# Second-layer keys made in the second attention from turned contexts kept in memory

## What is computed

```
x = x + tanh(g_xattn[0]) * attention0(layernorm(x), ctx)    # keys and values: context and own rows, masked
x = x + tanh(g_ffn[0])   * block0(layernorm(x))             # 8-bit rounding of rows and weights
x = x + tanh(g_xattn[1]) * attention1(layernorm(x), ctx)    # keys and values: context only
x = x + tanh(g_ffn[1])   * experts(layernorm(x))            # 2 of 8 experts a token, 256 -> 1024 -> 256
```

## Time and profile before

| | |
|---|---|
| median of 3 runs | 618.8 us (612.36 to 625.53) |
| profiled execution | 618.93 us |
| its span, first to last instruction | 617.2 us |
| busy: PE, DVE, ACT, POOL | 493.9, 424.3, 302.2, 162.2 us |
| first attention, steps of rounds 0 to 7 | 54.8 to 239 us |
| second attention, steps of rounds 0 to 7 | 328 to 438.8 us |
| bytes read and written in memory | 48.59 and 15.92 MB |

### The profile page before, as it was taken

How to read it: one execution, slowest core, us unless ns; L and a number is a source line. 1 busy time by engine, 2 the same in 40 slices (tenths; PEclk the granted TensorE clock), 3 DMA queues, 4 the chain that set the end, 5 groups by cost and what they waited for, 6 DMA issues and landing times. The chain is left out here.

```text
span 617.2 us, 15503 instructions
## 1 busy us (share of the span) xinstructions
PE 493.9 (80%) x5419; PEld 348.6 (56%) x5419; DVE 424.3 (69%) x920; ACT 302.2 (49%) x499; POOL 162.2 (26%) x191
## 2 busy tenths in 40 slices
PE   3987888898898877665478989999663299999993
PEld 2565566666565565333234656666443287887882
DVE  8767867777677754777528768877469776566651
ACT  5557565556555374143344757776542133333331
POOL 4600211221222111120245111101231425545432
PEclk9997999999999779786586989999775599999998
DMA  9577654454376000000467999994383012222210
GB/s 256 132 140 144 183 127 107 117 141 94 85 171 181 5 27 1 1 1 0 115 118 193 169 164 180 173 159 154 106 308 123 25 36 36 41 47 40 46 21 0
DMA packets 73247, 64.31 MB, mean 104 GB/s; under 512 B 33326, under 2 KB 65750, under 8 KB 73190
## 3 DMA queue, kind: packets, MB, share of 16 engines
q1 hardware_dynamic: 62904, 41.68, 31.3%
q0 software_dynamic: 8224, 21.06, 13.7%
q10 hardware_dynamic: 2064, 0.81, 0.5%
HBM read 48.59 MB, written 15.92 MB: 105 GB/s over the span
## 5 line engine op out<-in xcount | busy, mean ns | idle before, releaser
L518 PEld LDWEIGHTS PS<-QS,KS 112*120 112x120 f16 (+2 forms) x896 | 81.0, 140 | 28.8 <-issue 10.7
L518 PE MATMUL PS<-QS,KS 112*120 112x100 f16 (+2 forms) x896 | 89.2, 224 | 7.5 <-ACT QS L590 5.5
L629 DVE CUSTOM_DVE_ANT_0 PS<-PS,maskv 100x461 f32<-100x461 f32 x118 | 74.3, 647 | 14.7 <-PE PS L480 14.3
L632 DVE TENSOR_REDUCE mx<-PS 100x1 f32<-100x361 f32 x128 | 63.8, 529 | 30.0 <-PE PS L483 28.4
L581 ACT ACTIVATE PT<-PS 120x400 f32<-120x400 f32 (+1 forms) x128 | 63.3, 502 | 42.6 <-PE PS L518 41.5
L581 ACT ACTIVATE PT<-PS,ctxb 120x400 f32<-120x400 f32 (+1 forms) x96 | 56.9, 594 | 32.1 <-PE PS L518 30.9
L861 POOL TENSOR_SCALAR_AFFINE_SELECT PT<-PT 100x400 f32<-100x400 f32 x32 | 17.3, 541 | 159.9 <-ACT PT L581 159.9
L2173 PE MATMUL PS<-aT,WE 128*128 128x128 f16 x960 | 59.1, 223 | 0.0
L2173 PEld LDWEIGHTS PS<-aT,WE 128*128 x960 | 56.7, 100 | 0.1
L480 PE MATMUL PS<-KS,QS 65*100 65x461 f16 x118 | 44.9, 381 | 12.9 <-DVE mx L629 12.6
L2186 PE MATMUL PS<-WE,hidden_high 128*128 x160 | 53.0, 379 | 0.0
(11 more groups left out here) (322 smaller groups left out, 1050.2 us busy)
## 6 DMA issues: line engine op xcount, KB each, us to landing
share<-in_L_ffn_w_dram POOLq DMA_DIRECT2D x13, 1024.0 KB, 9.1
k_scratch<-share SPq DMA_DIRECT2D x32, 180.5 KB, 2.7
KS<-k_scratch SPq DMA_DIRECT2D x32, 180.5 KB, 3.9
KS<-k_scratch SPq DMA_DIRECT2D x64, 90.2 KB, 8.0
QS<-q_scratch SPq DMA_DIRECT2D x64, 50.0 KB, 2.8
v_scratch<-xn SPq DMA_DIRECT2D x8, 385.7 KB
values_staged<-v_scratch SPq DMA_DIRECT2D x8, 385.7 KB
WE<-in_L_ffn_w_dram POOLq DMA_DIRECT2D x2, 1024.0 KB, 8.7
```

What stands on the lines that cost most here:

```text
L518: last = nc.tensor.matmul(bank[0:kn, i * T:(i + 1) * T], KS[p][:, h, k0:k0 + kn], QS[p][:, h, :], start=True, stop=True)
L629: nc.vector.tensor_tensor_reduce(rows, rows, maskv[:, :], 1.0, -BIG, ALU.add, ALU.max, mx[p][:, h:h + 1]).then_inc(s_smf, 1)
L632: nc.vector.tensor_reduce(mx[p][:, h:h + 1], sm_bank[h % 2][0:T, 0:TC], X, ALU.max).then_inc(s_smf, 1)
```

## The change

The turned contexts (both halves, 361 KB a batch) are written to memory in the first attention, where the second layer's keys were written. In the first attention K2 and K3 are gone from set-up and rounds 0 to 5. For batches 0 and 1, whose second-layer keys must be there before the second attention, the turned context is read back into `cT[0]`, and the keys are made in round 6 (t=4, 5) and round 7 (t=1, 2). For batches 2 to 7 they are made in rounds 0 to 5 of the second attention, at t=0 and t=4, with ACT's half behind t=2 and t=5 and DVE's half behind the fifth and the eleventh maximum, from one buffer `cK`. SP writes them, waits until they have landed, and loads them back into the stack. Unread products are issued in these rounds only from t=8 on. Several tiles have new places. The loops over rounds are shorter by one turn in the second attention, with that turn's two rounds written out.

```diff
-        NV0, NK0, NW0 = 4, (2, 3, 6, 7), 8
-        TVK = {1: "T0", 2: "T1", 4: "K0", 5: "K1", 8: "V0", 9: "V1", 11: "K2", 12: "K3"}
+        NV0, NK0, NW0 = 4, (2, 3), 6
+        TVK = {1: "T0", 2: "T1", 4: "K0", 5: "K1", 8: "V0", 9: "V1"}
...
+        K17 = (1, 2)
...
+        def pe_K1b(pe, b, mb, n):
+
+            if mb == 0:
+                pe.wait_ge(s_c1, 16 * (b + 1))
+            pe.wait_ge(s_mf, n - 1)
+            pe_second_keys(pe, misc[KB[mb]][:, 0:TC], cT[0], mb).then_inc(s_md, 1)
...
         def act_hi_T(act, j, o, kc, n):
+            if o >= 2 and kc == 0:
+                act.wait_ge(s_cw[o % 2], 16 * (j + o // 2))
...
+        def sp_turned_out(sp, j, o):
+
+            sp.dma_start(c_dram[bass.ds(2 * j + o, 1)].rearrange("b p n -> (b p) n"),
+                         cT[o % 2][:, :, :, :].rearrange("p r k t -> p (r k t)")).then_inc(s_cw[o % 2], 16)
...
                     if keys:
+                        sp_turned_out(sp, j, u + 2)
...
-                        sp.wait_ge(s_mf, n0 + NK0[3] + 1)
-                        sp_keys_out(sp, j, u + 2, 1)
...
-                for p in range(2):
-                    sp.wait_ge(s_kw[1][p], KW * B // 2)
-                sp.dma_start(rd_[:, :, 0:NI], w_down.rearrange("(k p) n -> p k n", p=P)).then_inc(s_fw, 16)
-                round0(B // 2 - 1, 0, False, False, True)
+                sp.wait_ge(s_mf, N6)
+                sp.wait_ge(s_cw[0], 16 * B // 2)
+                sp_turned_in(sp, slice(0, 1), cT[0], s_c1)
+                sp.dma_start(rd_[:, :, 0:NI], w_down.rearrange("(k p) n -> p k n", p=P)).then_inc(s_fw, 16)
+                sp.wait_ge(s_mf, N6 + 2)
+                sp.wait_ge(s_cw[1], 16 * B // 2)
+                sp_turned_in(sp, slice(1, 2), cT[0], s_c1)
+                sp_keys_to(sp, 1, slice(0, 1), k1b[0], s_kw[1][0])
...
             @block.sync
             def _(sp):
+                sp_turned_in(sp, slice(2, 3), cK, s_ck)
...
+        K1T, K1H, K1L = (0, 4), (2, 5), (4, 10)
+        K1B = misc[1][:, 0:TC]
+
+        def pe_K1(pe, j, o, mb):
+
+            i = 2 * j + o
+            if mb == 0:
+                pe.wait_ge(s_ck, 16 * (i + 1))
+            if mb == 1 or not (isinstance(i, int) and i == 0):
+                pe.wait_ge(s_k1f, 2 * i + mb)
+            pe_second_keys(pe, K1B, cK, mb).then_inc(s_k1d, 1)
...
                     if keys:
-                        for g in range(H // HG):
-                            sp.wait_ge(s_std, STN + NST1 * i + 3 * (g + 1))
-                            sp_keys1(sp, j, u + 2, g)
-                            if g % 2 == 1:
-                                sp_queries_in(sp, j, u + 2, g // 2)
+                        for mb in range(KC):
+                            sp.wait_ge(s_k1f, 2 * i + mb + 1)
+                            sp.dma_start(k_dram[1][bass.ds(i + 2, 1), mb * HM:(mb + 1) * HM, :, :, :].rearrange(
+                                "b h d s t -> (b h d) (s t)"), k1d[p][:, mb, :, :].rearrange("p s t -> p (s t)")
+                                ).then_inc(s_k1w[mb], 16)
+                            if mb == 1 and more:
+                                sp_turned_in(sp, bass.ds(i + 3, 1), cK, s_ck)
+                            sp.wait_ge(s_k1w[mb], 16 * (i + 1))
+                            if mb == 1:
+                                sp_queries_in(sp, j, u + 2, 0)
+                                sp.wait_ge(s_std, STN + NST1 * i + 9)
+                            sp_keys1(sp, j, u + 2, 2 * mb)
+                            sp.wait_ge(s_std, STN + NST1 * i + 6 * (mb + 1))
+                            sp_keys1(sp, j, u + 2, 2 * mb + 1)
+                        sp_queries_in(sp, j, u + 2, 1)
...
                         pe_ST(pe, j, o, t, 1, STN, 2 * B)
-                        unread()
+                        if keys and t == K1T[1] + 4:
+                            pe.wait_ge(s_k1f, 2 * (2 * j + o) + 2)
+                        if not keys or t >= K1T[1] + 4:
+                            unread()
```

More of the change, by code:

```diff
@@ L772, in round0 @@
                     p = u % 2
-                    if ctx or weights:
+                    if keys:
                         sp.wait_ge(s_mf, n0 + 2)
@@ L923, in _ @@
                     act_hi_K(act, 0, 1, k, 6 + k)
-                for o in range(2):
-                    for k in range(2, 4):
-                        act_hi_K(act, 0, o, k, 6 + 2 * o + k)
                 act.wait_ge(s_small, 16 * 9)
@@ L954, in round0 @@
                         act_exp(act, j, u, t, 0, 0)
+                        if nxt and not keys and kind_of(t)[:1] == "K":
+                            act_hi_K1b(act, 0, int(kind_of(t)[1]), N6 + int(kind_of(t)[1]))
+                        if weights and t in K17:
+                            act_hi_K1b(act, 1, K17.index(t), N7 + K17.index(t))
                         if t == NT2:
@@ L1018, in _ @@
                     pe_K(pe, 0, 1, k, 6 + k, 5, True)
-                pe.wait_ge(s_wf, 8)
-                for k in range(2, 4):
-                    pe_K(pe, 0, 0, k, 6 + k, 1)
                 pe.wait_ge(s_kz, 1)
@@ L1071, in round0 @@
                             pe_K(pe, j, u + 2, int(kind[1]), n0 + NK0[int(kind[1])], n0 + 1, True)
+                        elif nxt and kind[:1] == "K":
+                            pe_K1b(pe, 0, int(kind[1]), n0 + int(kind[1]))
+                        elif weights and t in K17:
+                            pe_K1b(pe, 1, K17.index(t), N7 + K17.index(t))
                         elif nxt and kind[:1] == "V":
@@ L1157, in _ @@
                     dve_lo_K(dve, 0, 1, k, 6 + k, 6 + k)
-                for k in range(2, 4):
-                    dve_lo_K(dve, 0, 0, k, 6 + k, 6 + k)
                 dve.wait_ge(s_zero, 1)
@@ L1783, in _, with round1 @@
                 act_max_rows(act, 0, 0, 0, 2 * B)
-                def round1(j, o, first, nxt, e, m, full):
+                def round1(j, o, first, keys, nxt, e, m, full):
                     for t in range(NST1):
@@ L1789, in round1 @@
                             act_evac(act, j, o - 1, NBN)
+                        if keys and t in K1H:
+                            act_hi_K1(act, j, o, K1H.index(t))
                         if t in HIT1:
@@ L1828, in _, with round1 @@
                 pe_N(pe, 0, 0, 0, SMN)
-                def round1(j, o, first, nxt):
+                def round1(j, o, first, keys, nxt):
                     h = HA
@@ L1845, in round1 @@
                             h += 1
+                        if keys and t in K1T:
+                            pe_K1(pe, j, o, K1T.index(t))
                         if t == NT2_1:
@@ L1877, in _, with round1 @@
                 dve_step_low(dve, E - 1, 0, 1, stg[1])
-                def round1(j, o, first, nxt, e, m):
+                def round1(j, o, first, keys, nxt, e, m):
                     for h in range(HA, HA + H):
```

208 lines of the change are left out of this document (139 added, 69 removed).

## The result

The changed kernel takes 649.5 us (median of four runs, 641.5 to 651.9), against 620.0 for the kernel before beside it: a ratio of 1.048, 95% interval 1.030 to 1.065, slower. The forecast was 630.0, slower too, with a range that ends at 648.0. In the profiled execution 650.1 us stand against 618.9, 31.2 more. Of these, 6.0 are there when the second attention begins (334.0, before 328.0), and 25.2 come in it and behind it.

A forecast was written before the change was run, and what follows sets the result against it. PE was taken to set the first attention's rounds, PE and full transfers the second's. First half -13.2 - 2.0 + 3.9 + 1.3 = -10.0, second attention +21: 618.9 - 10 + 21 = 630 us, range 611 to 648.

The forecast's parts named there:

- Six rounds lose 2.2 each: First attention, six rounds without two key products: t=11 to t=15 in 3.6 us for 5.8, 13.2 less in all.
- Set-up, 2.0 less: Set-up before the first round: two batches lose two key products each, shortening DVE's chain by 2.0 us.
- ACT's wait before it overwrites a turned context is for a write issued two rounds (45 us) earlier: nothing: First attention: the wait for the turned context's write to land was to cost nothing, the write being long issued.
- Round 6, +3.9: First attention, round 6: PE stalls 2.7 us at t=4 for batch 0's context, plus 1.2 for DVE's two halves.
- Round 7, +1.3: First attention, round 7: context there early, DVE's halves cost 1.3 us, between 0 and 3.
- Second attention, +21: Second attention: the loop through the context and late last queries add 21 us in all.
- Five issues of 0.48, 2.4; and two landings: Second attention, context loop: 4.2 from product to stored half, 2.4 of issues, two landings of 5.2, 17.0 us a round.
- By throughput 16.3: Second attention: 0.74 MB more a round costs 3.0 us on top of 13.3, so 16.3 a round.
- The 3.9 of reserve: Second attention: a weight load is used 3.9 us after it lands, slack taken off the throughput cost.
- Short landings: Rival, second attention: writes land in 2.4 us, loop 11.4, rounds stay at 13.0, total 609 us; chance 0.15.
- The clock: Rival, second attention: PE's waits lower its clock, 2.4 us more in each of five rounds, total 642; chance 0.17.
- The first attention: Rival: DVE paces t=11 to t=15, a round gains only 1.2 us, six rounds 7.2, total 636; chance 0.10.

The follow-up runs named there:

- written_early: The changed kernel with the turned contexts of batches 0 and 1 written right behind the first keys of each, not behind both stack loads: 635.7 us, 1.031.
- reload_apart: The changed kernel with the contexts of batches 0 and 1 loaded back before round 4 into buffers of their own, not in round 6: 639.1 us, 1.035.
- context_after_product: The changed kernel with the second attention's next context asked for right behind the first write, once the second product is taken: 643.2 us, 1.038.
- issues_in_gaps: As context_after_product, with SP issuing both writes and the context before waiting for the first landing, first queries behind two key groups, loop written out: 631.0 us, 1.020.
- all_mended: The changed kernel with the edits of written_early, reload_apart and issues_in_gaps together: 614.1 us, 0.995 of the kernel before.
- two_banks: all_mended with a round's two key products at t=0 and t=3 in a bank each, copies behind the evacuation and at t=6: 615.5 us, 0.994.
- twelve_unread: The changed kernel with unread products at all twelve steps of a second-attention round again, keys made in the neighbouring bank: 649.0 us, 1.051.
- transfers_alone: The kernel before with the changed kernel's extra second-attention transfers added, to and from spare memory, nobody waiting for them: 628.6 us, 1.015.
- values_behind_write: The changed kernel with the load of the staged values issued behind a round's first write of keys, not ahead of it: 638.6 us, 1.026.

## Why the prediction was right or wrong

By its own terms, against the 31.2 us of the profiled executions:

- *Six rounds lose 2.2 each.* Right for rounds 1 to 5: 101.3 us for 113.3, 2.4 each, with t=11 to t=15 in 3.4.
- *Set-up, 2.0 less.* Round 0 began 4.6 earlier (50.2 for 54.8), in written_early 2.3. Right in sign, too small by 2.6 here.
- *"ACT's wait before it overwrites a turned context is for a write issued two rounds (45 us) earlier: nothing."* This is the step that failed most. It holds from round 2 on. For batches 0 and 1 there are no two rounds before: their write stands at the end of the set-up's queue, is issued 5 us after ACT wants it landed (56.55, and ACT idles from 51.7), and takes 6. Forecast -2.2 for round 0, measured +8.5: 10.7 us of the 20.2 that were missed. written_early shows it: moved ahead, round 0 takes 20.4.
- *Round 6, +3.9.* The wait was foreseen at its place; the load took 6.1 in place of 3.7, and the round cost 6.3. The term was too small by 2.4.
- *Round 7, +1.3.* Steps t=0 to t=5 took 1.4 longer than before, but up to t=15 4.7 with a lower clock (0.67 for 0.75). reload_apart tells what belongs to what: without the wait in round 6, rounds 6 and 7 take 2.4 more than before, as DVE's halves were to cost (1.2 and 1.3). The wait, with what follows it in round 7, cost the other 8.6 of 11.0, where the forecast had 2.7. Then the gated block took 3.1 more, for which the forecast had nothing; no run settles these.
- *Second attention, +21.* Measured 25.2, the size nearly right, the mechanism only half. "Five issues of 0.48, 2.4; and two landings" was the sum of a loop through the context, 17.0. That loop is there and sets every second round: from 378.44 to 397.22 it takes 18.8, with landings of 5.8 and 3.5 (forecast 5.2 each), issues of 3.1 between them (2.4), and 6.3 from the context's landing to the stored half (4.2). The other rounds were set by SP's own line: all 16 issues of a round (8.6) stand in one line with both landings. The text named what is queued behind the waiting instruction on SP, and did not add it up. In the round shown SP goes on 6.1 and 3.1 us after the two writes' issues. context_after_product takes the context out of the loop and leaves the round at 17.9; issues_in_gaps takes the wait out of the line and brings 14.2. So 21 came near 25.2 partly by luck: the line that was not added up is about as long as the loop that was.
- *By throughput 16.3.* Wrong, and that it agreed with 17.0 was chance: the same traffic runs in rounds of 14.2 at a share of 0.84 (all_mended), and of 13.4 at 0.80 (two_banks). Its 13.3 for a round before is from no row; rounds 1 to 6 average 13.7. The 3.9 of reserve is read rightly, although a weight load is used one round after its issue, not two as said ahead of the prediction: 387.13 lies in round 4, 405.58 in round 5.
- *The rivals.* Short landings: half true; 23 of 40 loads of keys landed in 2.1 to 2.8, and the first write, behind the staged values, still took 6. The clock: it fell as described (0.70 to 0.75 in long rounds), but by twelve_unread it cost little by itself. The first attention gained what was forecast.

Sum of the misses (in us): set-up -2.6, round 0 +10.7, rounds 1 to 5 -1.0, rounds 6 and 7 +5.8, the gated block +3.1, the second attention +4.2; together 20.2, the way from +11.0 to +31.2.

## What to carry to other kernels

When a change puts a wait into a queue that issues transfers, add up the whole round of that queue, every issue and every landing that it waits for, and compare that with the round of the engine that sets the pace. A wait for "the last use, two rounds ago" has to be looked at in the first rounds too, where the last use is the set-up's and stands at the end of its queue. If the sum is too long, move the wait behind the issues that don't need it before taking any transfer away.

## What the runs showed of the hardware

A DMA share of 1.0 did not mean that no more bytes could go through. At 1.02 the kernel before moved 180 GB/s; transfers_alone moved 209 at 1.05, issues_in_gaps 215 at 0.84. The share counts the time that packets are under way, and that grew: SP's packets took 61 ns each in the full stage (6842 in 67.0% of 39.1 us of 16 engines) and 40 ns in the first attention (8927 in 48.5% of 46 us), at 571 and 607 bytes each. So the share alone does not show the room; the bytes per second have to be read with it.

What a small transfer takes depends on what else is under way. In the changed kernel four loads of keys from 366.18 on, with no weight load in flight, landed in 2.3 to 2.4; the last ones of that round, issued from 374.47 on beside a load of 1 MB (373.85 to 381.17), in 5.7 to 6.7. The Trainium skill ("DMA: Bandwidth & Descriptors", section "Queues, rings and completion order") says that a DMA engine takes packets in turn from the queues that have work, which would slow such a transfer and not stop it; the trace fits, but no run was made for it alone. A load in front in the same queue counts too: in values_behind_write the first writes took 4.5 on average for 6.2, about half of what they had lost against the second writes (3.1).
